# Float8 rounding with magic numbers from an Abs, a residual sum and a normalisation by tiles, and a last store in halves

## What is computed

```python
def attn(x, w):       # both are rounded to float8_e4m3fn and scaled back
    xq = q(x, amax over 128 features of a token)      # q(v) = fp8(v * 448/safe) * safe/448
    wq = q(w, amax over a block of 128x128)
    return einsum('emk,enk->emn', xq, wq)
x = x + tanh(g_xattn) * attn(layernorm(x), ctx)
h = layernorm(x)
x = x + tanh(g_ffn) * (sum over the best 4 of 8 experts of comb * (silu(h@wg.T) * (h@wu.T)) @ wd.T
                       + sigmoid(h@sg.T) * (silu(h@swg.T) * (h@swu.T)) @ swd.T)
```

## Time and profile before

| | |
|---|---|
| median of 3 runs | 175.09 us (174.53 to 175.18) |
| the profiled execution | 174.99 us, span 172.8 us |
| TensorE busy | 154.2 us (89%) |
| VectorE, ScalarE, GpSimd busy | 123.2, 103.9, 81.1 us |
| granted TensorE clock | full in all 40 slices of the page |

### The profile page before, as it was taken

How to read it: one execution, slowest core, us unless ns; L and a number is a source line. 1 busy time by engine, 2 the same in 40 slices (tenths; PEclk the granted TensorE clock), 3 DMA queues, 4 the chain that set the end, 5 groups by cost and what they waited for, 6 DMA issues and landing times.

```text
span 172.8 us, 2338 instructions
## 1 busy us (share of the span) xinstructions
PE 154.2 (89%) x700; PEld 122.6 (71%) x700; DVE 123.2 (71%) x258; ACT 103.9 (60%) x223; POOL 81.1 (47%) x103
## 2 busy tenths in 40 slices
PE   0033979999999999999999999999999999999991
PEld 0022447787888887877788888888888888888880
DVE  1899882897779889988989667943486655444553
ACT  2588843578668699656375545884654444554530
POOL 4350564245673565563346444353665554444410
PEclk9999999999999999999999999999999999999999
DMA  4499920000499994134423325205999100000003
GB/s 129 130 392 402 399 101 0 2 4 4 113 277 236 351 401 176 23 114 133 154 83 119 79 70 206 95 4 106 265 246 334 52 4 0 0 0 2 0 0 121
DMA packets 12768, 23.00 MB, mean 133 GB/s; under 512 B 3266, under 2 KB 4290, under 8 KB 12756
## 3 DMA queue, kind: packets, MB, share of 16 engines
q1 hardware_dynamic: 12180, 22.34, 41.1%
q10 hardware_dynamic: 576, 0.52, 1.1%
HBM read 21.51 MB, written 1.09 MB: 131 GB/s over the span
## 4 chain that ended last, share of the span: by engine, by line
PE 83%; DVE 6%; ACT 2%; POOL 2%; DMA 2%; issue 2%; DVEq 1%; POOLq 0%
PE bank L1143 52%; PE bank L1248 4%; PE bank L1252 4%; PE bank L1250 4%; PE bank L1249 4%; PE bank L1255 4%; PE bank L1256 4%; DMA x<-xs 2%; PE bank L1119 1%; POOL rstd L350 1%; DVE amax_x L777 1%; PE bank L1265 1%; POOL x L356 1%; ACT xc L461 1%; ACT y L486 1%
## 5 line engine op out<-in xcount | busy, mean ns | idle before, releaser
L362 POOL TENSOR_TENSOR w_lo<-w_raw,w_hi 128x512 fp32r<-128x512 f32 (+1 forms) x33 | 41.6, 1260 | 49.9 <-ACT w_hi L531 49.9
L1143 PE MATMUL bank<-h_hi,w_hi 128*128 128x512 f32 x130 | 51.5, 396 | 0.0
L1143 PE MATMUL bank<-h_hi,w_lo 128*128 128x512 f32 x130 | 50.7, 390 | 0.0
L1143 PE MATMUL bank<-h_lo,w_hi 128*128 128x512 f32 x130 | 50.6, 390 | 0.0
L552 ACT ACTIVATE a_hi<-bank 128x512 fp32r<-128x512 f32 (+1 forms) x34 | 20.3, 598 | 33.8 <-DVE bank L897 33.3
L375 POOL TENSOR_TENSOR w_lo<-w_raw,w_hi 128x256 fp32r<-128x256 f32 x33 | 24.8, 751 | 13.8 <-ACT w_hi L535 13.7
L906 DVE TENSOR_TENSOR a_lo<-bank,a_hi 128x512 fp32r<-128x512 f32 x32 | 22.0, 688 | 10.2 <-ACT a_hi L552 10.0
L897 DVE TENSOR_TENSOR bank<-silu,bank 128x512 f32<-128x512 f32 x32 | 22.2, 695 | 9.4 <-PE bank L1143 7.4
L1143 PEld LDWEIGHTS bank<-h_hi,w_hi 128*128 128x128 f32 x130 | 24.4, 188 | 5.8 <-issue 0.7
L1143 PEld LDWEIGHTS bank<-h_hi,w_lo 128*128 128x128 f32 x130 | 24.4, 188 | 5.2
L1143 PEld LDWEIGHTS bank<-h_lo,w_hi 128*128 128x128 f32 x130 | 24.4, 188 | 4.7
(11 more groups left out here) (162 smaller groups left out, 210.9 us busy)
## 6 DMA issues: line engine op xcount, KB each, us to landing
w_raw<-w_full SPq DMA_DIRECT2D x32, 384.0 KB, 7.7
mix_b<-rows_dram SPq DMA_DIRECT2D x8, 256.0 KB, 6.5
out_t<-fin SPq DMA_DIRECT2D x4, 256.0 KB, 2.1
mix_b<-rows_dram SPq DMA_DIRECT2D x4, 224.0 KB, 6.1
mix_b<-rows_dram SPq DMA_DIRECT2D x4, 192.0 KB, 5.9
mix_b<-rows_dram SPq DMA_DIRECT2D x4, 160.0 KB, 5.8
x<-xs SPq DMA_DIRECT2D x2, 256.0 KB, 6.7
cw<-ctx_t SPq DMA_DIRECT2D x2, 256.0 KB, 7.0
```

The source lines that it names most:

```text
L362: nc.gpsimd.tensor_tensor(w_lo[:, n % 2, 0:cols], w_raw[:, n % RING, 0:cols], w_hi[:, n % 2, 0:cols].bitcast(F32), ALU.subtract).then_inc( ...
L1143: last = nc.tensor.matmul(out, w[k][a], x_of[k][b], start=(start and k == 0 and i == 0), stop=(stop and k == blocks - 1 and i == 2))
```

## The change

Four things are changed.

1. The magic number is now 2^20 times the value's magnitude, rounded to bf16, in new tiles `xm` and `cm`. ScalarE makes it with one Abs straight from the scaled value; the clip from below is a max inside the two instructions of VectorE. The masks on VectorE go. Context 0 keeps a mask and a multiplication on VectorE. `rounded` gives the negative value for x and for the context.
2. The residual sum of batch 0 on GpSimd is two instructions, one for each tile, and bn_stats of a tile waits for its tile alone.
3. The transposes of batch 1's second layer norm go tile by tile, and those of the first tile wait for its normalisation alone (`y2_first`).
4. The last unit's down products are finished for OUT[0] first; the last output is made in a piece of 128x512 and two of 128x256, and the last of these is stored from ScalarE's queue.

```diff
+            def magic_x(b):
+                a.wait_ge(x_scaled, b + 1)
+                nc.scalar.activation(xm[:, tile_slice(b)], xc[:, tile_slice(b)], ACT.Abs, scale=MAGIC).then_inc(magic_done, 1)
...
             centre(1)
+            magic_x(0)
             a.wait_ge(gates_landed, 32)
             nc.scalar.activation(g_tanh[:], g_raw[:], ACT.Tanh).then_inc(tanh_done, 1)
-            magic_x(0, 1)
             scale_ctx(0)
             scale_x(1)
+            magic_x(1)
             scale_ctx(1)
-            magic_x(1, 2)
+            magic_ctx(1)
             copy_xqt(0)
-            magic_ctx(1, 1)
             high_gu(0)
             copy_xqt(1)
             residual0(0)
...
+            def power_of_two_ctx0():
+                v.wait_ge(ctx_scaled, 1)
+                val, mag, _ = views_ctx(0)
+                after(did(nc.vector.tensor_scalar(c_exp[:].bitcast(I32), val.bitcast(I32), EXP_BITS, None, ALU.bitwise_and)))
+                after(did(nc.vector.tensor_scalar(mag, c_exp[:], 1.5 * MAGIC, LEAST * MAGIC, ALU.mult, ALU.max)))
+
+            def rounded(views, magics, done):
+                val, mag, out = views
                 v.wait_ge(magic_done, magics)
-                after(did(nc.vector.scalar_tensor_tensor(val, power, LEAST, val, ALU.add, ALU.add)))
-                nc.vector.scalar_tensor_tensor(out, val, LEAST, power, ALU.subtract, ALU.subtract).then_inc(done, 1)
+                after(did(nc.vector.scalar_tensor_tensor(val, mag, LEAST * MAGIC, val, ALU.max, ALU.add)))
+                nc.vector.scalar_tensor_tensor(out, mag, LEAST * MAGIC, val, ALU.max, ALU.subtract).then_inc(done, 1)
...
-                nc.gpsimd.tensor_tensor(x1[:, tile_slice(0), :], x1[:, tile_slice(0), :], y2[:, tile_slice(0), :], ALU.add)\
-                    .then_inc(x1_ready[0], 1)
+                for j in tiles(0):
+                    nc.gpsimd.tensor_tensor(x1[:, j, :], x1[:, j, :], y2[:, j, :], ALU.add).then_inc(x1_ready[0], 1)
...
+                if b == 0:
+                    for jj, j in enumerate(tiles(0)):
+                        v.wait_ge(x1_ready[0], jj + 1)
+                        step = did(nc.vector.bn_stats(bn[:, 1, j, :], x1[:, j, :]))
...
-                pe.wait_ge(y2_ready, b + 1)
-                for k in range(KC):
-                    for jj, j in enumerate(tiles(b)):
-                        last = nc.tensor.transpose(Y2T1[k][:, jj * P:(jj + 1) * P], y2[:, j, k * P:(k + 1) * P], eye[:])
-                    last.then_inc(y2t_psum, 1)
+                pe.wait_ge(y2_first, 1)
+                for jj, j in enumerate(tiles(b)):
+                    if jj == 1:
+                        pe.wait_ge(y2_ready, b + 1)
+                    for k in range(KC):
+                        done = nc.tensor.transpose(Y2T1[k][:, jj * P:(jj + 1) * P], y2[:, j, k * P:(k + 1) * P], eye[:])
+                        if jj == 1:
+                            done.then_inc(y2t_psum, 1)
...
+            def finish_last(added):
+                after(added[0])
+                v.wait_ge(out_done, 4 * KC - 1)
+                nc.vector.scalar_tensor_tensor(fin[:, 0, :], OUT[0][:], g_tanh[:, 1:2], x1t[:, 0, HN:T], ALU.mult, ALU.add)\
+                    .then_inc(fin_done, 1)
+                after(added[1])
+                v.wait_ge(out_done, 4 * KC)
+                for half in range(2):
+                    cols = slice(half * S, (half + 1) * S)
+                    nc.vector.scalar_tensor_tensor(fin[:, 1, cols], OUT[1][:, cols], g_tanh[:, 1:2],
+                                                   x1t[:, 1, HN + half * S:HN + (half + 1) * S], ALU.mult, ALU.add)\
+                        .then_inc(fin_done, 1)
...
             down_block(n - 2, 1)
             down(n - 1)
-            down(n)
+            down_block(n, 0, stop=True)
+            down_block(n, 1, stop=True)
```

More of the change, by code:

```diff
@@ L295, in _ @@
                 load_w(n)
-            for k in range(KC):
-                sp.wait_ge(fin_done, KC + k + 1)
-                sp.dma_start(out_t[k, :, HN:T], fin[:, k, :]).then_inc(stored, 16)
-            sp.wait_ge(stored, 16 * HALVES * KC)
+            sp.wait_ge(fin_done, KC + 1)
+            sp.dma_start(out_t[0, :, HN:T], fin[:, 0, :]).then_inc(stored, 16)
+            sp.wait_ge(fin_done, KC + 2)
+            sp.dma_start(out_t[1, :, HN:HN + S], fin[:, 1, 0:S]).then_inc(stored, 16)
+            sp.wait_ge(stored, 16 * (HALVES * KC + 1))
         @block.gpsimd
@@ L307, in _ @@
             nc.gpsimd.memset(halves[:, 0, :], -0.5)
-            nc.gpsimd.memset(halves[:, 1, :], 0.5)
-            nc.gpsimd.memset(least[:], -LEAST).then_inc(least_filled, 1)
+            nc.gpsimd.memset(halves[:, 1, :], 0.5).then_inc(factors_filled, 1)
             pool.wait_ge(ident_filled, 1)
@@ L462, in scale_x, with magic_ctx @@
                 last.then_inc(x_scaled, 1)
[L464 to L474, removed]
+            def magic_x(b):
+                a.wait_ge(x_scaled, b + 1)
+                nc.scalar.activation(xm[:, tile_slice(b)], xc[:, tile_slice(b)], ACT.Abs, scale=MAGIC).then_inc(magic_done, 1)
+            def magic_ctx(b):
+                a.wait_ge(ctx_scaled, b + 1)
+                nc.scalar.activation(cm[:, b], cw[:, b], ACT.Abs, scale=MAGIC).then_inc(magic_done, 1)
             def copy_xqt(b):
@@ L675, in _ @@
                 unit(n)
+            a.wait_ge(fin_done, KC + 3)
+            a.dma_start(out_t[1, :, HN + S:T], fin[:, 1, S:HN]).then_inc(stored, 16)
         @block.vector
@@ L767, in round_ctx, with flat @@
[L767 to L773 removed]
+            def flat(t):
+                return t.rearrange("p a b c -> p (a b c)")
@@ L815, in stats_x1 @@
             def stats_x1(b):
-                v.wait_ge(x1_ready[b], 1)
-                moments(1, x1, b, mean1_ready)
+                if b == 0:
+                    for jj, j in enumerate(tiles(0)):
+                        v.wait_ge(x1_ready[0], jj + 1)
+                        step = did(nc.vector.bn_stats(bn[:, 1, j, :], x1[:, j, :]))
+                else:
+                    v.wait_ge(x1_ready[b], 1)
+                    step = None
+                moments(1, x1, b, mean1_ready, step)
                 v.wait_ge(mean1_ready, b + 1)
@@ L826, in norm_x1 @@
                                                    ALU.subtract, ALU.mult)
+                    if b == 1 and j < BT * b + 1:
+                        last.then_inc(y2_first, 1)
                 last.then_inc(y2_ready, 1)
@@ L1060, in _ @@
                 unit(n)
-            finish(1, shared_1)
+            finish_last(shared_1)
         @block.tensor
@@ L1258, in down, with down_block @@
                     done.then_inc(out_done, 1)
-            def down_block(n, k):
+            def down_block(n, k, stop=False):
                 pe.wait_ge(d_lo_done, n + 1)
+                pe.wait_ge(a_hi_done, n + 1)
+                nc.tensor.matmul(OUT[k][:], d_hi(n, k), a_hi[:, a_slot(n), :], start=False, stop=False)
+                nc.tensor.matmul(OUT[k][:], d_lo(n, k), a_hi[:, a_slot(n), :], start=False, stop=False)
                 pe.wait_ge(a_lo_done, n + 1)
-                for w, act in ((d_hi(n, k), a_hi), (d_lo(n, k), a_hi), (d_hi(n, k), a_lo)):
-                    nc.tensor.matmul(OUT[k][:], w, act[:, a_slot(n), :], start=False, stop=False)
+                done = nc.tensor.matmul(OUT[k][:], d_hi(n, k), a_lo[:, a_slot(n), :], start=False, stop=stop)
+                if stop:
+                    done.then_inc(out_done, 1)
             def unit(n):
```

102 lines of the change are left out of this document (32 added, 70 removed).

## The result

The changed kernel has a median of 175.00 us over 22 executions (174.82 to 176.79), the kernel before, measured beside it, 174.87 us over 22 (174.53 to 175.43): ratio 1.0029, 95% interval 1.0016 to 1.0042. It is near that of the two means, 175.39 and 174.91 us (1.0027), and not that of the medians (1.0007). The forecast was 174.8, a gain of 0.16 us; measured is a loss, small but with an interval that leaves 1 out. The list of the 22 times says more than their median: 16 lie between 174.82 and 175.28 and have a mean of 174.98, and six lie between 176.0 and 176.79. The kernel before has nothing above 175.43. So there are two things to find: why the ordinary executions win nothing, and what the six are.

What follows compares the result with a forecast made beforehand. TensorE's unbroken 142 us of products was taken as the bound, so only front and end could move the time: +0.09 - 0.25 = -0.16 us against the profiled 174.99 gave 174.8 us, range 174.1 to 175.5.

Steps and rivals of the forecast that it cites:

- What bounds the kernel: TensorE's 142 us of unbroken products bounds the time; only the front before it and the end after it can move it.
- The rounding, +0.40: Front: two Abs on ScalarE delay batch 0's copy and `attend`, so batch 1's transposes start 0.40 us later.
- The sum by tiles, -0.18: Front: GpSimd's residual sum in two pieces hides the first bn_stats beside the second piece, winning 0.18 us.
- The transposes by tiles, -0.13: Front: only the second tile's two transposes remain after the last normalisation, taking 0.13 to 0.17 us off.
- The front's sum: Rounding, sum and transposes together before the first products: 0.40 - 0.18 - 0.13 = +0.09 us, ends -0.1 to +0.35.
- The end, -0.25: After the last matmul: the last store has half the bytes, so its transfer ends 0.25 us sooner (0 to 0.45).
- the 171.9: End: about when the kernel before was taken to finish moving its stores, against 171.63 us with the halved last store.
- the range: Bounds for the measured median: 174.1 us for half of the faster case, 175.5 us on the other side.
- the faster one: Front: VectorE's rounding sets the path and its 0.7 us arrives whole; 173.7 us, half 174.3; chance 0.20 of over 0.5% faster.
- The slower one: Front: TensorE reaches its faster rate later, nine slow fillers cost up to 1.8 us; all nine: 175.9 us, chance 0.07.
- The end gives nothing: End: Abs cost as forecast, halved transfers as slow as whole ones; 175.1 us, a case of the forecast (no measurable change, 0.70).
- differences under 0.5%: Whole kernel: changes below 0.9 us were said to be what a measurement can't tell from none.

Runs made afterwards that it cites:

- e12: The changed kernel with only the Abs rounding and ScalarE's new order kept, sum, transposes and end as before: median 175.69 us, ratio 1.0028.
- e4: The changed kernel with GpSimd's residual sum of batch 0 in one instruction again: median 175.50 us.
- e16: The changed kernel with batch 0's copy early, five fillers instead of nine, no repeated TensorE waits, both outputs stored whole from SP: median 173.96 us, ratio 0.9933.
- e8: The changed kernel with batch 0's copy early, the end of the kernel before and five fillers instead of nine: median 174.25 us, ratio 0.9956.
- e10: The changed kernel with TensorE's old list at the end, the new stores in halves kept: median 175.46 us, ratio 1.0013.
- e3: The changed kernel with the end of the kernel before (interleaved down products, two whole stores from SP): median 175.06 us, ratio 1.0003.
- e9: The changed kernel run again without an edit, as a control: median 175.89 us, ratio 1.0044.
- e2: The changed kernel with batch 0's `copy_xqt` moved ahead of the second context's scaling on ScalarE: median 174.62 us, ratio 0.9994.
- e7: The changed kernel with batch 0's copy early and the end of the kernel before: median 174.59 us, ratio 0.9978.
- e1: The changed kernel run again without an edit, as a control: median 175.16 us, ratio 1.0016.
- e11: The changed kernel with TensorE's new list at the end, but two whole outputs stored from SP: median 175.11 us, ratio 1.0030.
- e13: The kernel before with six already satisfied waits added ahead of TensorE's last unit: median 175.00 us.

## Why the prediction was wrong

**What bounds the kernel**: right. The block is 143.0 to 143.1 us in all twenty profiles, whatever VectorE and ScalarE do inside.

**The rounding, +0.40**: the mechanism held by every row (Abs 0.63 against 0.65 taken, `attend` 16.27 against 16.20, transposes 17.10 against 17.02, sum 19.54 against 19.44; 0.05 of each difference is the later load). The size was 0.49 (e12). What was missed is the 0.08 that VectorE is late once the mask ahead of `blk_c` is gone: the context's scaling and the scaling of x behind it start 0.07 to 0.08 later after the load. The shorter Abs give part of it back, so that `attend` is 0.02 and the sum 0.05 behind the forecast. The prediction followed VectorE's durations and not its wait for TensorE.

The figure of the Trainium skill ("ScalarE: Activation LUTs", Rules for kernel authors), 0.72 us for 512 elements, is for an ACTIVATE with a pointer bias, and no row here contradicts it: the Relu of before, whose bias is `least`, took 0.70 us. The Abs is called without a bias and took 0.61 to 0.63.

**The sum by tiles, -0.18**: -0.22 (e4). **The transposes by tiles, -0.13**: -0.12 (e12, e4). The front's sum was +0.09, measured +0.15, inside the ends that were given.

**The end, -0.25**: this is the step that failed. VectorE did as forecast: its last half ends 170.47 - 169.49 = 0.98 us after the last matmul's finish, 0.96 was worked out, and 1.06 it was before. But the forecast let the last transfer land up to 0.32 us sooner because it has half of the bytes, and took 0.25. The rows say 2.1 to 2.2 us for 128 and for 256 KB: the last half lands no sooner after its issue than a whole output, and the tail is 3.51 against 3.52 us. The end gave 0.0 in place of 0.25.

The transfers show why. In 40 slices of 168 to 178 us, before and then after:

```profile
GB/s 0 0 0 0 0 0 0 0 0 0 303 385 369 377 377 287 0 0 0 0 0 0 0 0 0 66 0 0 0 0 0 0 0 0 0 0 0 0 0 0
```

```profile
GB/s 0 0 0 0 0 0 0 0 0 0 328 377 369 344 336 324 21 0 0 0 0 0 0 0 0 0 0 0 0 0 0 0 0 0 0 0 0 0 0 0
```

(the 66 is the packet of instructions at 174.3.) In both, the stores are one unbroken stream of 0.52 MB, about 1.5 us long. The last half stands behind the others in it, and halving it takes no bytes off the stream. By the prediction's own working the kernel before moves 0.64 + 0.64 us and the changed one 0.64 + 0.32 + 0.32, which is the same; the 171.9 against which it set its 171.63 is not worked out there.

The edit has two parts of opposite sign, which the prediction left unsaid. With OUT[0] first the last output ends 0.86 us after the last matmul's finish instead of 1.06 (e16 against e8), and the tail is 0.18 shorter (3.38 against 3.56). With the halves it ends after 1.19 us instead of 1.06 (e10 against e3), since two halves take VectorE 0.87 us and one piece 0.75, and the tail is 0.14 longer (3.73 against 3.59). These are four profiled executions, the tails good to 0.05; together the two parts about cancel, as the changed kernel's 0.98 us and 3.51 say.

**What no step had**: the high executions. The 22 times' mean is 0.48 us above that of before; the ordinary executions account for 0.06, six of 22 at 1.5 above them for 0.41. They are the larger part of the measured loss. No row of before has a packet amid the stores, but the page has the queue, and the rivals named no cost for a changed list of instructions. That the median stayed inside the range is partly luck: in e9, with six high of 12, it is 175.89 us and outside.

**The rivals**: the faster one asked for `copy_xqt` by 15.5 and got it in e2, e7 and e8 (14.19 in e7), by moving it and not by a shorter Abs. Its condition was put wrongly: 15.5 is only 0.07 before the forecast's own 15.57, and a copy at 15.64 brought nothing of the 0.7. The slower one, slow fillers, is real (3.83 us for nine in e7), but in the changed kernel it is covered: e1's nine took 3.21 us instead of 2.63, the wait for `y` is gone there, and its front is 17.66 all the same. "The end gives nothing", 175.1 us, was the nearest case. The sentence that differences under 0.5% can't be told from none asked too little of the measurement: with 22 executions each the interval is 0.13% to either side.

## What to carry to other kernels

When an instruction is removed from a waiting engine's list, look at what its time covered; and when work moves to another engine, look at what stands behind it in that list: one call moved two lines up brought 0.28 us in the front, and five fillers instead of nine 0.5 more. Before splitting a store, look whether the stores at the end form one stream: then smaller pieces take nothing off it, and what helps is an earlier first store (e16). And look at all execution times, not at the median alone: a cost that falls on one execution in four is invisible in most profiles, and needs the profile of a high one.

## What the runs showed of the hardware

A packet of instructions takes its turn on the same 16 DMA engines as the data. In the four profiled executions in which it fell amid the last stores, the last half landed 3.2 to 3.9 us after its issue instead of 2.1 (the two whole stores of e11 have a median of 3.3), and the tail was 1.1 to 1.8 us longer. Six satisfied waits in TensorE's list moved that packet by 5.4 us (e13).

The Trainium skill ("Runtime: NRT & Kernel Launch", Instruction fetch mechanics) says that each engine's instructions are refilled in blocks of 16 KiB over a DMA queue of its own, at a cost "mostly hidden". The size agrees with the trace (0.02 MB a packet). Hidden it is amid the products, where the block has the same length in every run, but not at the kernel's end.

TensorE's fillers of the same shape ran 0.22 or 0.43 us apart at a granted clock of 1.00, and how many were slow changed between executions of one kernel: nine took 2.63 us in the first profile of the changed kernel and 3.21 in e1. The factor of two is that between the clock's two levels, 2.4 and 1.2 GHz, but the granted clock in the rows shows no change, and what decides it wasn't tried.
